# Reordering the pooled scores, the weight broadcasts and the convolution filler in a two-attention and 3x3-convolution kernel

## What is computed

```python
x = x + attention(group_norm(x))     # half of the channels from 2x2 windows, half from pooled attention
x = x + conv3x3(relu(group_norm(x) * mask)) + bias
# windows: softmax over the 4 pixels of each 2x2 window, 4 heads of 32 channels, projection + bias
# pooled:  queries are all 1024 pixels, keys and values the 256 averaged windows, 4 heads,
#          out = softmax(q k^T * scale) v, projection + bias
# mask:    per channel, from the rounded centre of mass of the normalised image
```

## Time and profile before

| | |
|---|---|
| median of 3 runs | 397.45 us (396.68 to 397.61) |
| the profiled execution, its own time | 395.26 us |
| its span, first to last instruction | 393.4 us |
| granted TensorE clock, mean | 0.905 of full |

### The profile page before, as it was taken

The page is one execution under the profiler, slowest core; times in us unless marked ns, Lnnn a source line. Parts: engine busy times, 40 slices in busy tenths (PEclk is TensorE's granted clock), DMA queues, the critical chain, the costliest instruction groups (busy, mean ns, idle before and its releaser), DMA issues.

```text
span 393.4 us, 4166 instructions
## 1 busy us (share of the span) xinstructions
PE 334.0 (85%) x1546; PEld 235.9 (60%) x1546; DVE 305.2 (78%) x628; ACT 113.8 (29%) x124; POOL 101.5 (26%) x59
## 2 busy tenths in 40 slices
PE   2696667999578699998899869998899999898995
PEld 1485435257454475486668654586668755676884
DVE  4953659997876988789987876889889868988562
ACT  2322053142402536213215416224025431031200
POOL 0456999600084011000570010000850200010100
PEclk9788586899959599999699969998899999999999
DMA  7659600008700000039300400069000100101002
GB/s 248 239 75 127 213 4 0 2 0 108 92 2 5 0 0 2 0 93 127 36 5 0 160 2 0 2 120 129 6 5 0 55 0 1 55 0 53 2 0 107
DMA packets 10340, 20.39 MB, mean 52 GB/s; under 512 B 1872, under 2 KB 4816, under 8 KB 10064
## 3 DMA queue, kind: packets, MB, share of 16 engines
q1 hardware_dynamic: 10320, 20.13, 24.9%
HBM read 7.93 MB, written 4.19 MB: 31 GB/s over the span
## 4 chain that ended last, share of the span: by engine, by line
PE 47%; DVE 34%; issue 6%; DMA 6%; ACT 5%; SPq 1%; DVEq 0%
PE slot L940 20%; PE cps L972 13%; PE slot L1016 6%; PE cps L940 3%; DVE st L536 3%; DMA qs<-probs 3%; DVE l_max L695 3%; PE cps L1016 2%; DMA xy<-x 2%; ACT probs L470 1%; DVE v_lo L677 1%; DVE xn L918 1%; DVE xn L604 1%; DVE gn L564 1%; PE slot L1140 1%
## 5 line engine op out<-in xcount | busy, mean ns | idle before, releaser
L321 POOL TENSOR_TENSOR probs<-q_w,k_w 128x1024 f32<-128x1024 f32 x16 | 37.4, 2365 | 131.2 <-DVE rw L640 125.7
L972 PE MATMUL cps<-v_hi,cw_hi 128*128 128x512 f32 (+1 forms) x144 | 60.2, 418 | 6.5 <-DVE v_lo L677 3.9
L972 PE MATMUL cps<-v_hi,cw_lo 128*128 128x512 f32 (+1 forms) x144 | 60.1, 417 | 0.0
L972 PE MATMUL cps<-v_lo,cw_hi 128*128 128x512 f32 (+1 forms) x144 | 58.5, 406 | 0.0
L695 DVE TENSOR_REDUCE l_max<-slot 128x4 f32<-128x1024 f32 x32 | 37.5, 1220 | 18.8 <-PE slot L940 18.8
L940 PE MATMUL slot<-ks,qs 96*128 96x256 f32 x128 | 26.6, 360 | 19.5 <-DVE l_max L695 10.0
L470 ACT ACTIVATE probs<-slot 128x1024 f32<-128x1024 f32 x32 | 31.6, 1023 | 34.2 <-PE slot L940 34.0
L972 PEld LDWEIGHTS cps<-v_hi,cw_hi 128*128 128x128 f32 x144 | 29.2, 203 | 17.6 <-ACT v_hi L464 4.6
L940 PEld LDWEIGHTS slot<-ks,qs 96*128 96x128 f32 x128 | 23.1, 250 | 24.4 <-DVE l_max L695 15.1
L972 PEld LDWEIGHTS cps<-v_hi,cw_lo 128*128 128x128 f32 x144 | 28.9, 201 | 6.5 <-issue 0.7
L972 PEld LDWEIGHTS cps<-v_lo,cw_hi 128*128 128x128 f32 x144 | 28.9, 200 | 5.1
(11 more groups left out here) (163 smaller groups left out, 634.3 us busy)
## 6 DMA issues: line engine op xcount, KB each, us to landing
qs<-probs SPq DMA_DIRECT2D x24, 256.0 KB, 7.5
xy<-x SPq DMA_DIRECT2D x8, 512.0 KB, 8.3
out<-xy SPq DMA_DIRECT2D x8, 512.0 KB, 2.8
raw_cw<-conv_w SPq DMA_DIRECT2D x2, 1152.0 KB, 6.6
ks<-probs SPq DMA_DIRECT2D x12, 128.0 KB, 7.5
probs<-h_qkv SPq DMA_DIRECT2D x2, 192.0 KB, 4.6
probs<-l_kv SPq DMA_DIRECT2D x2, 128.0 KB, 4.2
probs<-selectors SPq DMA_DIRECT2D x1, 256.0 KB, 4.0
```

Of the source, the lines that this page charges most:

```text
L321: nc.gpsimd.tensor_tensor(qk[:, j].rearrange("p (n w) -> p n w", n=NW), q_w[:].rearrange("p (n w) -> p n w", n=NW), k_w[:, j * G:(j + 1) * ...
L972: ins = nc.tensor.matmul(cps[:, pos % 2, y0 * WT:y1 * WT], (cw_hi, cw_hi, cw_lo)[part][:, k, pos, dy + 1, o * P:(o + 1) * P], (v_hi, v_lo, ...
```

## The change

It touches `rest` on TensorE, the exponentials on ScalarE and the order of work on VectorE. The scores use slots 0 and 1 in turn (i % 2), and all four broadcasts use slot 2, each one waiting until VectorE has multiplied the one before it. In the code the broadcasts j = 0 to 3 stand between the scores 2 and 3, 3 and 4, 4 and 5, 5 and 6. The eight transposes of the softmax weights come first in `rest`, before score tile 2; ScalarE copies them after the exponential of tile 2 instead of tile 3. REST goes from (4, 3, 5, 3, 4, 8) to (4, 2, 1, 30): fewer convolution matmuls stand among scores and broadcasts, and 30 behind `lpv`. The tiny matmul of the group means moves behind the last exponential and writes slot 1. On VectorE the result of the convolution's sum (V_SUM), the late statistics and `of_groups` move behind the three additions, and the result of the difference (V_DIFF) behind L849.

```diff
-ST_SLOT = (0, 1, 0, 1, 1, 0, 2, 1)
-PB_SLOT = (0, 1, 0, 2)
-REST = (4, 3, 5, 3, 4, 8)
+REST = (4, 2, 1, 30)
...
-                exp_scores(b, range(2, LT - NW))
+                exp_scores(b, (2,))
                 act.wait_ge(pt_pe, b + 1)
                 nc.scalar.copy(p_w[:], flat[2]).then_inc(pt_act, 1)
-                exp_scores(b, range(LT - NW, LT))
+                exp_scores(b, range(3, LT))
...
                 for j in range(NW):
-                    if j == 2:
-                        if not first:
-                            conv_result(b - 1, (V_SUM,))
-                        if late:
-                            next_statistics()
-                        if not last:
-                            stats.of_groups()
                     dve.wait_ge(pb_pe, b * NW + j + 1)
...
                 nc.vector.tensor_tensor(q_w[:], pv[0], pv[2], ALU.add).then_inc(pv_dve, 1)
+                if not first:
+                    conv_result(b - 1, (V_SUM,))
+                if late:
+                    next_statistics()
                 if not last:
+                    stats.of_groups()
                     stats.scale_and_bias()
-                if not first:
-                    conv_result(b - 1, (V_DIFF,))
...
                 nc.vector.tensor_tensor(k_w[:], flat[0], v_w[:], ALU.mult).then_inc(lnorm, 1)
+                if not first:
+                    conv_result(b - 1, (V_DIFF,))
...
             def rest(b, first, last):
                 conv = NoConvolution() if first else Convolution(b - 1, EARLY)
-                conv.more(REST[0])
-                for i in range(2, LT - NW):
+                def scores(i):
                     pe.wait_ge(st_exp, b * LT + i - 1)
                     pooled_scores(b, i)
-                    conv.more(REST[1])
+
+                def values(j):
+                    wait_count(pe, pv_ready, b * NW + j if j else 0)
+                    for half in range(2):
+                        ins = mm(slot[2][:, half], sel[:, j], p_w[:, halves(half)], True, True)
+                    ins.then_inc(pb_pe, 1)
 
                 pe.wait_ge(soft_c, (b + 1) * N_SOFT)
...
                 ins.then_inc(pt_pe, 1)
-                conv.more(REST[2])
+                conv.more(REST[0])
+                scores(2)
+                conv.more(REST[1])
                 pe.wait_ge(pt_act, b + 1)
-                for j in range(NW):
...
-                    conv.more(REST[3])
-
-                for i in range(LT - NW, LT):
...
-                    pooled_scores(b, i)
-                    conv.more(REST[4])
+                for i in range(3, LT):
+                    if i - 3 < NW:
+                        values(i - 3)
+                    conv.more(REST[2])
+                    scores(i)
+                    conv.more(REST[2])
 
                 def window_out():
                     pe.wait_ge(pv_dve, (b + 1) * 2)
+                    if not last:
+                        pe.wait_ge(gn_c[0], (b + 1) * N_GN + GN_SENT + 1)
...
                 pe.wait_ge(st_exp, (b + 1) * LT)
                 if last:
                     window_out()
+                else:
+                    group_means(b + 1, 0)
+                pe.wait_ge(pv_ready, (b + 1) * NW)
                 by_head(2, lambda t, h: cst[:, C_ONE:C_ONE + HD], lden_pe)
...
-                conv.more(REST[5])
+                conv.more(REST[3])
```

More of the change, by code:

```diff
@@ L469, in exp_scores @@
                     act.wait_ge(st_pe, b * LT + i + 1)
-                    nc.scalar.activation(probs[:, i], flat[ST_SLOT[i]], ACT.Exp, scale=SCALE / NW)\
+                    nc.scalar.activation(probs[:, i], flat[i % 2], ACT.Exp, scale=SCALE / NW)\
                         .then_inc(st_exp, 1)
@@ L796, in step @@
                 late = b + 1 == RING
-                stats = Statistics(b + 1, 0)
+                stats = Statistics(b + 1, 0, to=1)
                 def next_statistics():
@@ L816, in step @@
                         pv[j].rearrange("p (n w) -> p n w", n=NW),
-                        flat[PB_SLOT[j]].rearrange("p (n w) -> p n w", n=NW),
+                        flat[2].rearrange("p (n w) -> p n w", n=NW),
                         v_w[:, j * G:(j + 1) * G].unsqueeze(1).to_broadcast([P, NW, G]),
@@ L993, in group_means @@
                 pe.wait_ge(gn_c[i], b * N_GN + GN_SENT)
-                mm(slot[2][:, 0, 0:2 * KT], cst[:, C_GRP:C_GRP + P], mv[i][:].rearrange("p k s -> p (k s)"),
+                mm(slot[1 if b and i == 0 else 2][:, 0, 0:2 * KT], cst[:, C_GRP:C_GRP + P], mv[i][:].rearrange("p k s -> p (k s)"),
                    True, True).then_inc(gn_pe[i], 1)
@@ L1035, in pooled_scores @@
                 for half in range(2):
-                    last = mm(slot[ST_SLOT[i]][:, half], ks[0:SM, h, t * P:(t + 1) * P], qs[0:SM, h, halves(half)],
+                    last = mm(slot[i % 2][:, half], ks[0:SM, h, t * P:(t + 1) * P], qs[0:SM, h, halves(half)],
                               True, True)
```

## The result

The changed kernel took 414.56 us in the median of 4 runs (413.28 to 417.37), the kernel before 397.06 us beside it (396.24 to 397.61). The ratio is 1.049 with an interval of 1.044 to 1.055: slower by 17.5 us in the medians, 19.6 us by the ratio. The forecast was 415.0 us in a range of 406 to 422.

A forecast was written before the change was run, and what follows sets the result against it. TensorE was taken to bound the changed stretches, so its added idle time counts: 1.1 + 4.5 + 4.5 + 4.6 (images 0 to 3) + 1.0 + 1.8 (clock) = 17.5 us on 397.45 gives 415.0 us, range 406 to 422.

The forecast's parts named there:

- Rival 1: Behind `lpv` VectorE or ScalarE sets the pace and hides TensorE's fillers: faster, 393.2 us; chance 7%.
- rival 2: Fillers pushed back meet TensorE's waits on VectorE in `front`: loss only 2 to 9 us, middle 403; chance 7%.
- Turned weights: Images 1 to 3: early transposes bring the first broadcast 0.6 to 0.7 us earlier; TensorE idles 1.9 us in image 1.
- The one bank: Rounds of images 1 to 3: broadcasts 2.1 us apart, TensorE idle 0.7 us three times, `lden` 10.1 us after first broadcast.
- One of the prediction's own signs of being wrong: Image 1: `lden` starting later than 152.4 + 1.1 would mean the rounds are dearer than thought.
- Images 1 to 3: Fillers owed behind `lpv` outweigh the earlier `lden` or window projection: 4.5, 4.5 and 4.6 us later.
- The step that called the wait moved and not removed: Image 2: TensorE still waits 4.8 us for the late statistics, now at the group means.
- Image 0: No filler, half clock, later copy, but quicker GpSimd: 1.1 us later, bounds 0 and 2.2.
- The failed step: Image 0: VectorE's additions and fifteen small instructions end the stage; ScalarE starts at 79, 1 us after 78.00.
- the first, 1.0 us for the rounds: Rounds of images 1 to 3: one slow clock spell of 3.5 us, costing 0.3 us an image, 1.0 in all.
- the second, 1.8 us at `lden` of images 1 and 3: A second slow clock spell at `lden`, 1.8 us in each of these images, so 0 to 3.5; 1.8 taken.
- The third rival: TensorE's clock stays at half through rounds and `lden` of images 1 to 3: about 423 us; chance 10%.

The follow-up runs named there:

- filler_back: Kernel before with REST = (4, 1, 2, 1, 1, 30), V_SUM behind the additions and V_DIFF behind L849: 405.78 us, ratio 1.024.
- copy_first: Changed kernel with ScalarE copying the turned weights ahead of the exponential of tile 2: 414.00 us, ratio 1.047.
- full_filler_copy: Changed kernel with REST = (4, 2, 3, 10), V_SUM between second and third multiplication, turned weights copied before tile 2's exponential: 399.29 us, ratio 1.008.
- second profile: The changed kernel, unchanged, run again beside the kernel before: 415.81 us, ratio 1.049.

## Why the prediction was right

**The bound.** Right. TensorE is busy without gaps behind image 1's `lden` in both kernels, and moving fillers, with the two results that follow them, cost 9.5 us by the ratio (filler_back). Rival 1, idle time behind `lpv`, and rival 2, waits in `front` that take up the fillers, are out: `front` took 38.3 and 37.7 us where it had taken 38.3 twice.

**Turned weights.** Right in size: TensorE was idle for 1.6, 1.9 and 1.9 us at the copy in images 1 to 3 (1.9 to 2.3 forecast). What it did not see is that in image 1 VectorE was the next in line, so that removing this wait was worth nothing there (copy_first), and 0.3 us with the rounds covered (full_filler_copy).

**The one bank.** Right: in image 1 broadcasts 2.05 to 2.12 us apart (forecast 2.1), each wait put down to L806, `lden` 10.0 us after the first broadcast (157.02 - 147.01; forecast 10.1). In images 2 and 3 up to two of the three rounds ran slow and took 2.3 to 2.7 us, the others 1.95 to 2.05. One of the prediction's own signs of being wrong did come if it is read by the clock: `lden` of image 1 at 157.02, later than 152.4 + 1.1. But the rounds are not dearer; the image itself began 4.9 us later (131.79 for 126.93), through image 0. The kernel before had three double banks in use for its broadcasts (`PB_SLOT`), not two as the prediction says; no number hangs on that. The cost lies in the idle time and not in the bank: covered, with the copy first, the changed kernel comes within 0.8% of before.

**Images 1 to 3.** Forecast 4.5, 4.5 and 4.6, measured 4.2, 4.4 and 5.2 (second profile 5.0, 5.0 and 4.3). In image 2 the wait was forecast at 4.8 us and showed 5.8: TensorE came to it 9.3 us after the first broadcast (forecast 10.0), the statistics were done at 15.1 (forecast 14.8). Half clock followed, as forecast: from the group means through `lpv` it took 10.98 us where the same 70 matmuls took 9.44 in image 1 (above), 1.5 us lost for 1.8 forecast:

```profile
245.74 10.98 PE slot L936 x70
```

The step that called the wait moved and not removed was right for the changed kernel. That the same move is worth 5.7 us with the fillers of the kernel before was not seen.

**Image 0.** Mis-sized: 1.1 us forecast, 5.6 us between the first two profiles. 2.5 us of it lie ahead of the transposes, where the chain is caught by GpSimd or not in either kernel (5.0 and 8.5 us in the two profiles of before, 7.5 and 6.8 in those of the changed kernel). From the transposes to the projections the two kernels take 28.4 and 27.3 us before and 31.5 and 32.7 after, so 3 to 5 us are the change's. The failed step is the one that let VectorE's chain end the stage ("the fifteen small instructions 2.9: ScalarE starts at 79, 1 us after 78.00"). ScalarE did start in time, 21.7 us after the transposes (80.23 - 58.50) for 21.4 before, and GpSimd was out of the way, as forecast: the additions took 1.23 us each. But `lden` came 4.3 us later behind the transposes than in the first profile of before, 1.8 of it at the late copy and the rest in the rounds. ScalarE's casts of the next input and VectorE's division wait for `lpv` behind it:

```profile
86.16 1.99 ACT L417 CAST xn_hi<-xn 128x1024 fp32r<-128x1024 f32 x2 [2.84 <-PE slot L936]
...
86.23 1.22 DVE L843 TENSOR_TENSOR k_w<-slot,v_w 128x1024 f32<-128x1024 f32 x1 [1.60 <-PE slot L936]
```

The chain of work doesn't pass through them. It stays on TensorE, from the group means through `lpv` and then through four matmuls (eight records) `cps<-cst` of `keep_warm`, whose result nobody reads; in `rest` they stand in image 0 alone, ahead of the last projection:

```profile
75.13 10.97 PE slot L936 x70
86.09 2.78 PE cps L936 x8
```

VectorE's division was done at 87.45 and that projection started at 88.71. In the first profile of before the same projection had waited 0.57 us for VectorE. So in image 0 the late `lden` decides, on TensorE, and not VectorE's chain. The half clock of the rounds (granted 0.50, 2.5 to 2.6 us each) was in the forecast; that nothing covers it in image 0 was not. No run takes out the `keep_warm` matmuls, so what they cost is open.

**The clock.** Of the two terms the first, 1.0 us for the rounds, was about right and the second, 1.8 us at `lden` of images 1 and 3, did not come. At full clock the three rounds of an image take 6.2 us. In the first profile those of image 1 did, those of images 2 and 3 were partly slow and took 6.7 and 7.0 (granted 0.82 up to the late wait and 0.85 up to the window projection): 1.5 us by the shortest case, 6.15. `lden` ran at full clock in images 1 and 3. In the second profile the rounds of images 2 and 3 took 6.15 us each, and image 1's, granted 0.83, took 7.5, 1.3 more than in the first:

```profile
146.30:156.50 10.20, 8.80 (x28) 6.02 (x28) 6.71 (x12) 4.24 (x5) 2.39 (x1) 0.83 0.00 0
```

Of the four timed runs the longest, 417.37 us, had a mean granted clock of 0.887, the shortest, 413.28, had 0.898. The third rival, half clock throughout, did not come: the spells end. The Trainium skill (TensorE: Matmul & The Clock Gate, A second HAM failure mode: psum-queue depth-cycling) tells of a kernel whose clock oscillated because TensorE idled briefly between groups of matmuls. The traces agree only in part: one or two slow spells in the rounds of images 1 to 3, worth 0.6 to 1.3 us each, and which image has one changes between two profiles of one kernel.

So the mechanism and the three middle terms were right. That the total met the medians, 17.5 us for 17.5, is luck: image 0 was too small by 2 to 4 us, the clock too large by 1.3 to 1.5, and the ratio gives 19.6.

## What to carry to other kernels

When an engine is busy to the last tenth in a stretch, count what is moved past a point (here 27 matmuls, 6.2 us) against the idle time at the place where it goes: single-buffering and a late copy cost little while other work covers them, and cost in full once that work has been moved behind them. A wait put behind independent work is a gain only if that work still stands there: moved behind the additions, the late statistics cost 1.5 us of waiting with the fillers in place and 5.8 with the fillers gone. Removing one wait tells little if the next engine is late by as much, so look for who would be waited for next, and for whose instructions it can collide with at its new place.

## What was not expected of the hardware

Instructions of VectorE on 2 elements or 128 elements that take 0.16 to 0.29 us alone took 1.8 us beside GpSimd's work on SBUF, and whether they were caught hung on 0.9 us in the start of the chain: two profiles of one unchanged kernel differ by 2.4 us in that stretch and by 0.1 us elsewhere. Nor does one idle stretch tell what TensorE's clock does next. In the first profile of the changed kernel it fell to half in the rounds of images 2 and 3, after idle stretches of 1.90 and 1.88 us at the copy, and not in those of image 1, after 1.56. In the second profile it was the other way round: no fall after 1.89 and 1.90 us in images 2 and 3, and a fall in image 1 at the second broadcast, after 1.56 us and then 0.94.
